# A graph network kernel: the sums' activation one unit later, the table's low half one chunk step earlier, row keys six units later

## The reference, cut to what matters

```python
h = jnp.maximum(_layernorm(x), 0.0)
x = x + relu(segment_sum((h * deg**-0.5)[src], dst)) @ W.T + b     # layer 0
h = jnp.maximum(_layernorm(x), 0.0)
src_h = h[src] @ W_msg.T + b_msg                                    # layer 1
messages = segment_sum(src_h + edge_embed[edge_type], dst)
x = x + _gru_cell(messages, h, W_ih, W_hh, b_ih, b_hh)
```

## Time and profile before

| | us |
|---|---|
| median of 3 runs | 945.72 |
| lowest and highest run | 945.04, 948.14 |
| the profiled execution | 946.63 |
| span of its trace | 944.9 |
| TensorE busy, weight loads | 850.7, 757.2 |
| VectorE busy | 781.7 |
| ScalarE busy | 505.0 |

### The profile page before, as it was taken

One profiled execution on the slowest core, in us unless ns is written; L12 is line 12 of the kernel. 1 busy time (PEld: TensorE's weight loads), 2 busy tenths in 40 slices (PEclk: granted clock), 3 DMA queues, 4 the chain that ended last, 5 costly groups with the idle time before them and its releaser, 6 DMA issues.

```text
span 944.9 us, 21128 instructions
## 1 busy us (share of the span) xinstructions
PE 850.7 (90%) x8962; PEld 757.2 (80%) x8962; DVE 781.7 (83%) x1144; ACT 505.0 (53%) x924; POOL 83.5 (9%) x76
## 2 busy tenths in 40 slices
PE   2253989999999999999999999899999999999995
PEld 2142878888888888888888888788898889888984
DVE  6798999999999999999999991386667666766885
ACT  1479678888888888888888884211101110111011
POOL 6880202020020100000000000000000000000000
PEclk9996899999999999999999999899999999999998
DMA  5532434345543345543335500656766677667650
GB/s 125 116 119 87 161 143 167 148 165 208 205 177 143 149 166 204 201 167 143 143 148 206 205 17 13 174 209 240 289 256 237 248 288 258 235 248 289 259 203 15
DMA packets 38597, 169.43 MB, mean 179 GB/s; under 512 B 8140, under 2 KB 21651, under 8 KB 35552
## 3 DMA queue, kind: packets, MB, share of 16 engines
q1 hardware_dynamic: 32188, 160.25, 45.0%
q0 software_dynamic: 6000, 6.48, 2.9%
q10 hardware_dynamic: 308, 1.28, 0.5%
HBM read 87.93 MB, written 80.00 MB: 178 GB/s over the span
## 4 chain that ended last, share of the span: by engine, by line
PE 59%; DVE 21%; ACT 12%; issue 4%; DMA 3%; POOL 1%; DVEq 0%; SPq 0%; POOLq 0%
PE ps L1271 27%; PE ps L1145 14%; DVE work L716 7%; PE ps L1134 7%; ACT ring L942 7%; DVE work L723 6%; PE ps L1237 2%; PE ps L1238 2%; DVE work L731 2%; DMA tab<-dst 1%; DMA tab<-dst,row_i 1%; PE ps L1157 1%; PE ps L1171 1%; ACT tab L953 1%; PE ps L1242 1%
## 5 line engine op out<-in xcount | busy, mean ns | idle before, releaser
L1134 PE MATMUL ps<-work 128*128 128x106 f16 x3125 | 429.5, 216 | 54.5 <-ACT ring L942 34.0
L1145 PE MATMUL ps<-ring,tab 125*128 125x250 f16 x2500 | 416.4, 273 | 0.6 <-ACT ring L947 0.6
L942 ACT ACTIVATE ring<-ps 128x848 f16<-128x848 f32 x375 | 329.3, 881 | 80.4 <-PE ps L1134 75.1
L1134 PEld LDWEIGHTS ps<-work 128*128 128x128 f16 x3125 | 287.9, 101 | 75.8 <-ACT ring L942 34.3
L1271 PE MATMUL ps<-ring,tab 125*128 125x250 f16 (+1 forms) x2500 | 277.0, 269 | 0.0
L1271 PEld LDWEIGHTS ps<-ring,tab 125*128 125x128 f16 (+1 forms) x2500 | 242.6, 97 | 28.8 <-issue 0.3
L1145 PEld LDWEIGHTS ps<-ring,tab 125*128 125x128 f16 x2500 | 245.1, 99 | 25.6 <-ACT ring L947 0.9
L716 DVE TENSOR_TENSOR work<-iota_row,mch 128x3150 f16<-128x3150 f16 x125 | 225.2, 1801 | 8.6 <-PE ps L1134 8.3
L723 DVE TENSOR_TENSOR work<-iota_w,mch 128x1250 f16<-128x1250 f16 x250 | 194.0, 818 | 0.0
L804 DVE TENSOR_TENSOR work<-work,ring 125x3250 f16<-125x3250 f16 (+1 forms) x92 | 161.7, 1779 | 0.3 <-DMA ring<-adjacency 0.3
L1085 ACT ACTIVATE raw<-ps,bg 128x250 f32<-128x250 f32 x50 | 20.7, 466 | 175.3 <-PE ps L1238 175.3
(11 more groups left out here) (166 smaller groups left out, 578.8 us busy)
## 6 DMA issues: line engine op xcount, KB each, us to landing
adjacency<-ring SPq DMA_DIRECT2D x23, 2937.5 KB
ring<-adjacency SPq DMA_DIRECT2D x46, 812.5 KB, 6.3
ring<-adjacency SPq DMA_DIRECT2D x46, 750.0 KB, 9.2
adjacency<-ring SPq DMA_DIRECT2D x23, 183.1 KB
h_turned<-hst SPq DMA_DIRECT2D x25, 125.0 KB, 2.1
raw<-h_turned SPq DMA_DIRECT2D x25, 125.0 KB, 2.1
out<-x_sb SPq DMA_DIRECT2D x25, 125.0 KB
x_sb<-x SPq DMA_DIRECT2D x3, 560.0 KB
```

The source lines that it names most:

```text
L942: act.activation(to(x * 2 * u, 2, x), ps[:, s:s + 2, 0:x * SLOTS].rearrange("p b (x h) -> p h b x", h=SLOTS), ACT.Copy).then_inc(sem("evac ...
L1134: last = pe.matmul(ps[:, 2 * (u % 2) + i // BANKW, o:o + WCOLS], lohot[:, s, k, :], combo[:, s, k, :], start=True, stop=True)
L1145: mm = pe.matmul(psD[c % 2], tabv[0][P, h, s, :], adj[c % 2][P, h, :], start=i == 0, stop=i == 2 * BLOCKS - 1)
```

## The change

Four things are moved; no instruction is added or taken away. ScalarE's L967 goes from before a chunk's unit 0 to behind it. TensorE's `post0_low_tensor` goes from window 6 of the next chunk to window 121 of the same chunk, and ScalarE's `post0_low_scalar` from behind unit 0 of the next chunk to behind unit 15 of the same. TensorE's `post0_x_tensor` goes from window 14 to window 22. `row_keys` goes from behind unit 1 to behind unit 7. VectorE's order stays as it was.

```diff
             for c in range(CHUNKS):
-                if c >= 2:
-                    post0_aggr_scalar(act, c - 2)
...
-                    if c >= 2 and c % AHEAD == 2 and c + AHEAD + 1 < CHUNKS and u == 1:
+                    if c >= 2 and c % AHEAD == 2 and c + AHEAD + 1 < CHUNKS and u == 7:
                         row_keys(act, c + AHEAD + 1, min(AHEAD, CHUNKS - c - AHEAD - 1))
...
                     if c >= 2:
-                        if u == 0 and c >= 3:
-                            post0_low_scalar(act, c - 3)
+                        if u == 0:
+                            post0_aggr_scalar(act, c - 2)
...
+                        if u == UNITS - 1:
+                            post0_low_scalar(act, c - 2)
-            post0_low_scalar(act, CHUNKS - 3)
             post0_scalar(act, CHUNKS - 2)
...
-        POST0 = {14: post0_x_tensor, 89: post0_turn_tensor, 104: post0_table_tensor}
+        POST0 = {22: post0_x_tensor, 89: post0_turn_tensor, 104: post0_table_tensor, 121: post0_low_tensor}
...
-                    if c >= 3 and w == 6:
-                        post0_low_tensor(pe, c - 3)
                     if c >= 2 and w in POST0:
                         POST0[w](pe, c - 2)
...
-            post0_low_tensor(pe, CHUNKS - 3)
```

## The result

| | before | after |
|---|---|---|
| median of 22 runs each | 947.59 us | 945.87 us |
| lowest and highest | 944.89, 949.36 | 943.99, 946.78 |
| ratio, 95% interval | | 0.9981 [0.9973, 0.9989] |
| span of the profiled execution | 944.9 | 944.3 |

The changed kernel is 1 to 2.6 us faster. The forecast was 4.0 us slower; the time lies inside the range that was given, with the sign wrong. The median before is 1.9 us higher here than the 945.72 of the three runs that the forecast was added to, so the time alone says little and the ratio is what counts.

The account below looks back on a forecast made before the run. VectorE and TensorE were near their limits, linked by the post0 chain; later `psX` was to cost 2.65 + 0.25 + 1.00 + 0.10 = +4.0 us on 945.72, giving 949.7 us. Its range was 943.5 to 952.8 us.

Parts of the forecast that it names:

- The chain: In each chunk `psX` holds L739, then batch 4, `pnm` and L984; the next chunk starts 7.79 us behind L984.
- Rival A: `psX` does not hold VectorE, so the freed time comes back: -5.3 us, 940.4 us; chance 0.13.
- The place of `psX`: Time from chunk start until VectorE can take `psX`, used as +3.75 us; VectorE itself is ready at +3.08 or +3.21.
- ten pairs: TensorE from the first product matmul to the one behind window 22, 0.16 us a pair, 1.59 us unrounded.
- unit 15's copy: Before the chunk start, with the low half's matmul at window 121: the copy starts some 0.05 us later.
- L739 to `pnm`: On VectorE with nothing waited for: 4.75 us from L739 to batch 4, then 3.93 us to `pnm` in chunk 13.
- The sum: +0.53 us for each three chunks from 4 to 18, 2.65; plus 0.25, 1.00 and 0.10 for other chunks: +4.0 us.
- rival B: Loss and gain cancel with `psX` at +3.45 to +3.65 us: 945.7 to 948.2 us; chance 0.25.
- L1177 at window 121: The low half's matmul on TensorE costs 0.13 us and does not stall for `tab_hi`, whose margin is 0.12 us.
- Window 23: On TensorE behind L1157, whose wait for L1003 goes: expected to start 0.32 us earlier.
- Row keys: 0.66 us of ScalarE move to behind unit 7, before L984 in chunk 14: costs and brings nothing.
- The sum of 0: By the rule alone: VectorE has 98% against TensorE's 86%, so a gap closed on TensorE alone is worth nothing.

Follow-up runs that it names:

- The sweep over windows: Changed kernel with post0_x_tensor behind window 18, 20 or 26 in place of 22: ratios to the kernel before 0.9933, 0.9935 and 1.0122.
- window 18: Changed kernel with post0_x_tensor behind window 18 in place of 22, nothing else: ratio to the kernel before 0.9933.
- the last kernel: Kernel before with post0_x_tensor behind window 17, post0_norm_vector behind batch 3 (was 4), post0_std_scalar behind unit 3 (was 5): ratio 0.9864.
- windows 17 and 26: post0_x_tensor behind window 17 (was 14) on the kernel before: ratio 0.9926; behind window 26 (was 22) on the changed kernel: 1.0122.

## Why the prediction was wrong in sign

**The chain: right.** L739 waits for `psX` in chunks like 13 and 15, batch 4 no longer waits, L984 waits for `pnm` in every chunk (22 waits of 0.34 to 0.83 us in chunks 3 to 24), and the next chunk starts 7.79 us behind it. The sweep over windows confirms it. Rival A's numbers for a `psX` that is early, 19.72 us for a chunk like 13 and 60.38 for a trio, are met by window 18 with 19.69 (349.81 - 330.12) and 60.35.

**The place of `psX`: the term that failed.** It was worked out as +3.76 and used as +3.75; it is +3.56 (337.06 - 333.50). Its five parts:

| part | forecast | measured |
|---|---|---|
| chunk start to the first product matmul | 1.16 | 334.62 - 333.50 = 1.12 |
| ten pairs | 1.59 | 336.21 - 334.62 = 1.59 |
| to the start of L1157 | 0.19 | 336.31 - 336.21 = 0.10 |
| to the end of L1159 | 0.78 | 337.02 - 336.31 = 0.71 |
| to the start of L739 | 0.04 | 0.04 |

The two parts of L1157 are wrong by 0.16 together. The other 0.04 is the first part: unit 15's copy was taken to start later, and did not. The 0.78 was read where L1157 had just waited, and was used where no wait is left. The 0.19 is in no row of L1157. Another fp32 group of before, L1171, has it behind its matmul, and there it is a wait for ScalarE:

```profile
329.24 0.37 ACT L993 ACTIVATE hst<-ps 128x250 f32<-128x250 f32 x1
329.47 0.27 PE L1145 MATMUL ps<-ring,tab 125*128 125x250 f16 x1
329.66 0.51 PEld L1171 LDWEIGHTS ps<-wm_sb,hst 128*125 128x125 f32 x4
329.66 0.38 PE L1171 MATMUL ps<-wm_sb,hst 128*125 128x128 f32 x1
```

L1171 reads `hst`, which L993 writes until 329.61. Its weight load starts 0.05 behind that, and not together with the matmul in front, as that of L1156 does at 336.21. No idle time is drawn, since the matmul in front is drawn until 329.74.

The trace of before had L1157 itself without a stall; in chunk 2 L1157 follows its matmul (108.39) by 0.11 us and L1159 ends 0.70 us after its start:

```profile
108.39 0.27 PE L1145 MATMUL ps<-ring,tab 125*128 125x250 f16 x1
108.50 0.60 PE L1157 MATMUL ps<-w_sb,aggr 128*125 128x128 f32 x4
108.93 0.27 PE L1159 MATMUL ps<-b_parts,onesb 65*125 65x256 bf16 x1
```

**L739 to `pnm`: 8.56, not 8.68.** An L739 that has waited is drawn shorter than one directly behind L731, and what follows it comes sooner: batch 3 starts 338.21 - 337.06 = 1.15 behind it, not 1.25 as in 336.44 to 337.69 before. That is 0.10 of the 0.12; from batch 3 to the end of `pnm` it is 345.62 - 338.21 = 7.41, where 7.43 was reckoned. A row of the trace of before, at the end of the build, had the short form:

```profile
578.49 0.42 DVE L739 TENSOR_TENSOR x_sb<-ps,x_sb 125x256 f32<-125x256 f32 x1 [10.79 <-PE ps L1159]
```

**The sum.** Both errors count in every chunk that `psX` sets: 0.19 + 0.12 = 0.31 us, twice in a trio, 0.62 of the 0.67 us by which the trio was missed. Over the 21 chunks the forecast was +4.0 and the traces give -0.97, a miss of 5.0 us: five trios 3.35, chunk 3 0.32 (20.75 forecast, 20.43 measured), chunks 19 to 23 1.37 (20.26 forecast each; 19.94, 19.99, 20.10, 19.95 and 19.95 measured). So 0.3 us in a chain that runs 16 times turned the sign, and it took both errors: by the prediction's own sum a `psX` at +3.56 alone gives 4.0 - 16 x 0.19 = +1.0 us, and the 0.12 behind L739 another 16 x 0.12 = 1.9 less. The prediction had this amplification in its text, 1.6 us for 0.1 us of `psX`, and then gave the place of `psX` a spread of 0.14 us downward, from 3.75 to 3.61, where the error was 0.19. It also gave rival B too little: B was drawn for exactly this place, +3.45 to +3.65, and for this reason, a place of L1157 taken 0.1 to 0.3 us too late. B comes nearest to what happened, a difference below the 2.8 us that the prediction called none; it had 0 to 2.5 us slower, since the 0.12 behind L739 is not in it.

**The other steps.** L1177 at window 121 did not wait, as said: it starts at 332.59, 0.11 behind its matmul at 332.48. Unit 15's copy was to start 0.05 later; from that copy to the chunk start it is 333.50 - 333.26 = 0.24 us against 333.36 - 333.11 = 0.25 before, so no shift is seen there. Window 23 was to start 0.32 us earlier in its chunk; it starts 0.51 earlier, at 336.87 - 333.50 = 3.37 in place of 337.24 - 333.36 = 3.88, mostly because of the same two terms of L1157. Row keys cost nothing, as said. The rule of the Trainium skill that was weighed ("Perfetto Trace Analysis", section "Identifying the Most-Contended Engine"), to work first on the engine with the highest occupancy, names VectorE here, and the last kernel, with VectorE busy 59.25 of 59.60 us, agrees. The sum of 0 that the prediction drew from it holds only for an edit that leaves VectorE's waits alone: windows 17 and 26 give -0.7% and +1.2% against the kernel before, and no instruction is added or taken away.

## What to carry to other kernels

When a step is moved on one engine, look up who takes its result and with how much slack; here it was 0.31 us, and the move was 0.75. If engines run in a ring, write the ring as one sum from chunk start to chunk start, count how often each term goes round, and take each term from a row in the same condition (after a wait or not) as it will have. A wait need not be drawn as idle time: compare when the weight load starts, too. Then try the place itself: one number, window 17, gives 0.7% where the whole change gives 0.2%, and asking what waits next gave another 0.6%, perhaps in part by the clock of chunk 2.

## What the runs showed of the hardware that had not been expected

A matmul group can wait without any idle time in the trace, and its weight load tells. Where the weight load of L1157 (fp32, two matmuls drawn as four) starts together with the 250-column matmul in front, as at window 22, the group starts 0.10 to 0.11 us behind that matmul and is drawn 0.60 us long. Where the load had to wait for ScalarE, it starts 0.03 us (before, 335.32) or 0.05 us (window 17, 333.09) ahead of the group, and the group is drawn 0.67 and 0.66 us long.

VectorE's fp32 add of 125 x 256 (L739) is drawn 0.42 us long behind a wait and 0.53 directly behind L731. Directly behind L562, a short instruction of 0.17 us, it is 0.43 without a wait (360.81, in the run with L739 behind batch 3). So the difference hangs on the instruction in front, not on the wait.

In chunk 2 the granted clock of TensorE was 0.50 for some 3 us in six of eleven traces and 1.00 in the others, worth 1.2 to 1.4 us from L984 to the next chunk start. None of this shows in an engine's busy time, and the first two mattered for this forecast.
